# Routing weights of an expert layer: spread over the partitions by a DRAM round trip instead of TensorE products

## The reference

```
logits = gelu(xf @ w_r1 + b_r1) @ w_r2 + b_r2
probs = softmax(logits)
top_p, top_i = top_k(probs, 2);  top_p = top_p / sum(top_p)
v = 0;  integrated = xf
for _ in range(2):
    ctx = concat(integrated, v)
    shared: ctrl -> (x_shared, v_shared) by _inl
    per chosen expert: hidden = gelu(ctx @ w1[e] + b1[e]); ctrl = hidden @ w2[e] + b2[e]
                       (x_r, v_r) = _inl(ctrl, integrated, v, mu), weighted by top_p and summed
    x_next = sw * x_shared + (1 - sw) * x_r;  v_next likewise
    halt = sigmoid(gelu(x_next @ w_h1) @ w_h2); refined = gelu(x_next @ w_f1) @ w_f2
    integrated += halt * refined * integration_weight;  v = v_next

_inl: alpha, beta, gate = sigmoid, softplus, sigmoid of the thirds of ctrl
      v_next = alpha * v - beta * (x - mu);  x_next = x + 0.1 * gate * v_next
```

## Time and profile before

| | before |
|---|---|
| median of 3 runs | 743.63 us |
| lowest and highest | 735.77, 746.27 us |
| the profiled execution | 746.65 us |
| its span | 744.9 us |
| TensorE busy | 688.9 us (92%) |
| VectorE busy | 560.3 us (75%) |
| ScalarE busy | 489.3 us (66%) |
| GpSimd busy | 215.0 us (29%) |
| moved by DMA | 31.81 MB in 20987 packets |

### The profile page before, as it was taken

How to read it: one execution, slowest core, us unless ns; L and a number is a source line. 1 busy time by engine, 2 the same in 40 slices (tenths; PEclk the granted TensorE clock), 3 DMA queues, 4 the chain that set the end, 5 groups by cost and what they waited for, 6 DMA issues and landing times.

```text
span 744.9 us, 14725 instructions
## 1 busy us (share of the span) xinstructions
PE 688.9 (92%) x4872; PEld 368.8 (50%) x4872; DVE 560.3 (75%) x1749; ACT 489.3 (66%) x1342; POOL 215.0 (29%) x197
## 2 busy tenths in 40 slices
PE   6999999799999998999699999999979999989997
PEld 3655566466566432333245566655335665563332
DVE  4789898779998578677956999976038888845663
ACT  3778894389996688588857999834666666523201
POOL 2614662371444277336713032331000000000000
PEclk9899999899999989999899999999999999999999
DMA  5786000175000000000001600000000000000500
GB/s 204 158 253 259 1 3 1 33 162 127 3 2 2 2 0 1 0 2 0 0 22 45 128 2 2 2 29 1 0 0 1 1 2 1 0 1 1 227 2 28
DMA packets 20987, 31.81 MB, mean 43 GB/s; under 512 B 1648, under 2 KB 17968, under 8 KB 20272
## 3 DMA queue, kind: packets, MB, share of 16 engines
q1 hardware_dynamic: 20912, 30.86, 14.5%
HBM read 23.22 MB, written 7.63 MB: 41 GB/s over the span
## 4 chain that ended last, share of the span: by engine, by line
PE 69%; DVE 16%; ACT 8%; issue 5%; DMA 1%; POOL 1%; DVEq 0%; ACTq 0%; SPq 0%
PE bank L1137 12%; PE bank L1378 9%; DVE RING L1940 5%; PE bank L1408 4%; PE bank L1251 4%; PE bank L1540 4%; PE bank L1238 4%; DVE RING L1952 4%; PE bank L1327 4%; PE bank L1265 3%; PE bank L1527 3%; PE bank L1388 2%; PE bank L1740 2%; PE bank L1713 2%; PE bank L1158 2%
## 5 line engine op out<-in xcount | busy, mean ns | idle before, releaser
L938 ACT ACTIVATE RING<-RING,NMX 128x256 f32<-128x256 f32 x384 | 190.9, 500 | 25.8 <-DVE NMX L1940 24.1
L1940 DVE CUSTOM_DVE_ANT_0 RING<-bank,ADJM 128x256 f32<-128x256 f32 x384 | 145.5, 418 | 19.6 <-PE bank L1327 16.6
L1378 PE MATMUL bank<-W,RING 128*128 128x128 f32 x768 | 118.5, 287 | 5.4 <-ACT RING L950 5.1
L1378 PEld LDWEIGHTS bank<-W,RING 128*128 128x128 f32 x768 | 83.6, 144 | 52.9 <-ACT RING L938 41.5
L1952 DVE COPY RING<-bank 128x512 f32<-128x512 f32 x144 | 98.6, 686 | 5.6 <-PE bank L1378 5.2
L618 POOL TENSOR_TENSOR SUMS<-SUMS,small 128x8 f32<-128x8 f32 x36 | 59.2, 1644 | 127.0 <-ACT RING L938 127.0
L576 POOL TENSOR_TENSOR small<-small 128x2 f32<-128x2 f32 (+2 forms) x17 | 19.4, 1138 | 215.0 <-DVE small L1798 214.9
L938 ACT ACTIVATION_READ_ACCUMULATOR RING<-RING,NMX 128x1 f32 x384 | 72.8, 189 | 0.0
L852 ACT ACTIVATE RING<-bank,NMX 128x512 f32<-128x512 f32 x64 | 43.4, 684 | 39.1 <-DVE NMX L1882 29.2
L1882 DVE TENSOR_REDUCE NMX<-bank 128x1 f32<-128x512 f32 x64 | 39.8, 683 | 31.4 <-PE bank L1238 31.3
L1540 PE MATMUL bank<-ARENA,W 64*128 64x512 f32 x180 | 60.5, 669 | 2.3 <-DVE ARENA L2168 1.9
(11 more groups left out here) (265 smaller groups left out, 1241.3 us busy)
## 6 DMA issues: line engine op xcount, KB each, us to landing
ARENA<-scratch SPq DMA_DIRECT2D x12, 384.0 KB, 7.0
ARENA<-wrows SPq DMA_DIRECT2D x8, 512.0 KB, 7.5
scratch<-ARENA SPq DMA_DIRECT2D x18, 192.0 KB, 2.8
W<-in_weights SPq DMA_DIRECT2D x1, 2564.0 KB, 22.7
ARENA<-scratch SPq DMA_DIRECT2D x12, 192.0 KB, 3.7
scratch<-ARENA SPq DMA_DIRECT2D x18, 128.0 KB, 6.7
W<-in_weights SPq DMA_DIRECT2D x2, 1024.0 KB, 14.3
W<-in_weights SPq DMA_DIRECT2D x1, 1905.5 KB, 15.4
```

Of the source, the lines that this page charges most:

```text
L938: nc.scalar.activation(P_OF(n)[:, q * S:(q + 1) * S], S_OF(n)[:, q, :], ACT.Exp, bias=NMX[:, 2 * t + q:2 * t + q + 1], scale=-1.0, accum_o ...
L1378: mm = nc.tensor.transpose(bk[:, o:o + P], P_OF(n)[:, i:i + P], ident)
L1940: nc.vector.tensor_tensor_reduce(out=S_OF(n)[:, q, :], in0=SBANK(n)[:, q * S:(q + 1) * S], in1=ADJM[:, b, q, :], scale=-1.0, scalar=BIG, o ...
```

## The change

The three-part split, the selector products and their bank ring are gone. VectorE writes the weights once, in fp32, into `WT1` ordered by expert. One product with the identity turns them (64 rows of 128), `spread` is one copy of 64x128 into `WT1T`, SP writes that to a new DRAM tensor `wrows1` and reads rows back, broadcast over the 128 partitions: for each half-pass p and expert e one DMA of 512 tokens (128 x 512 fp32, 256 KB) into one of eight SBUF buffers `WROW1[e]`, 32 DMAs in all. The buffers are places whose contents are no longer needed (parameters of the first two attentions, `XN`, two of the bias matrices). For p of 1 and more each DMA waits until the multiply of the half-pass before has read the buffer. `first` and `scaled` read the weights from SBUF after waiting for `s_w1[e]`. The remaining entries of TensorE's list keep their order; `RB_AT` follows the count of banks.

```diff
-        WROW = RING[:, 12, :].bitcast(BF16)
-        WBF = small[:, 540:572].bitcast(BF16).rearrange("p (t e) -> p t e", t=NT)
+        WT1 = small[:, 640:704]
+        WT1T = RING[0:NE * NT, 12, 0:P]
+        WROW1 = ([w("wk0", i * 512, i * 512 + 512) for i in range(4)]
+                 + [XN[:, 4 * i:4 * i + 4, :].rearrange("p t d -> p (t d)") for i in range(2)]
+                 + [ADJ[:, i, :, :].rearrange("p q k -> p (q k)") for i in range(2)])
...
@@ block.sync
             write_keys(2)
+            sp.wait_ge(s_eb, RB_AT[2] - NC)
+            sp.dma_start(wrows1, WT1T).then_inc(s_w1dram, 16)
+            sp.wait_ge(s_w1dram, 16)
+            first_rows = wrows1.rearrange("(e t) j -> e (t j)", e=NE)
+            for p in range(2 * NC):
+                for e in range(NE):
+                    if p >= 1:
+                        sp.wait_ge(s_t1[p - 1] if p <= NC else s_tt[p - 1], nth(e))
+                    sp.dma_start(WROW1[e], first_rows[e:e + 1, half(p % NC)].to_broadcast([P, 512])).then_inc(s_w1[e], 16)
             sp.wait_ge(s_int, 2 * NC)
...
@@ block.tensor
                 pe.wait_ge(s_wt, 1)
-                for c in range(NC):
-                    bk = rb.fill(pe)
-                    for i in range(4):
-                        mm = nc.tensor.transpose(bk[0:3 * NE, i * P:(i + 1) * P], XN[:, 4 * c + i, 0:3 * NE], ident)
-                    mm.then_inc(s_fb, 1)
-
-            def weights(p, es):
-
-                for e in es:
-                    bk = rw.fill(pe, s_t1[p] if p < NC else s_tt[p], nth(e))
-                    nc.tensor.matmul(bk[:, :], ROWS[0:3 * NE, e * P:(e + 1) * P], WROW[0:3 * NE, half(p % NC)],
-                                     start=True, stop=True).then_inc(s_fw, 1)
+                bk = rb.fill(pe)
+                nc.tensor.matmul(bk[0:NE * NT, 0:P], WT1, ident, start=True, stop=True).then_inc(s_fb, 1)
...
             gates(0, (NE,))
-            pe.wait_ge(s_eb, rb.n)
-            weights(0, (0, 1))
             gates(0, (0, 1))
-            weights(0, (2, 3))
             gates(0, (2, 3, 4, 5))
-            weights(0, (4, 5))
...
@@ block.vector
-            link(nc.vector.scalar_tensor_tensor(WT8, EXPL, 1.0, SEL, ALU.add, ALU.mult))
-
-            for i in range(3):
-                link(nc.vector.tensor_copy(WBF, WT8))
-                part = nc.vector.tensor_copy(XN[:, :, NE * i:NE * (i + 1)], WBF)
-                if i < 2:
-                    link(part)
-                    link(nc.vector.tensor_tensor(WT8, WT8, XN[:, :, NE * i:NE * (i + 1)], ALU.subtract))
-            part.then_inc(s_wt, 1)
+            nc.vector.scalar_tensor_tensor(WT1.rearrange("p (e t) -> p t e", e=NE), EXPL, 1.0, SEL, ALU.add,
+                                           ALU.mult).then_inc(s_wt, 1)
 
             def spread():
 
-                for c in range(NC):
-                    nc.vector.tensor_copy(WROW[0:3 * NE, half(c)], rb.take(dve)[0:3 * NE, :]).then_inc(s_eb, 1)
+                nc.vector.tensor_copy(WT1T, rb.take(dve)[0:NE * NT, 0:P]).then_inc(s_eb, 1)
+
+            def weight(p, e):
+
+                dve.wait_ge(s_w1[e], 16 * (p + 1))
+                return WROW1[e]
...
             def first(p, es):
-                        wgt = rw.take(dve)
+                        wgt = weight(p, e)
                         dve.wait_ge(s_sp[p], nth(e))
                         nc.vector.tensor_tensor(sp, sp, wgt[:, :], ALU.mult).then_inc(s_t1[p], 1)
...
             def scaled(p, es):
-                        wgt = rw.take(dve)
+                        wgt = weight(p, e)
```

## The result

| | before | changed |
|---|---|---|
| median of 4 runs | 744.95 us | 752.61 us |
| lowest and highest | 735.77, 753.55 | 748.55, 756.49 |
| the profiled execution, its span | 746.65, 744.9 us | 756.49, 754.7 us |

A forecast was written before the change was run, and what follows sets the result against it. The routed layer was taken to have no single bound: ScalarE, VectorE and TensorE each fill one window. Terms +3.1 -3.9 -0.5 +1.5 +1.5 = +1.7 us gave 745 us from the median 743.63; range 734 to 757.

The forecast's parts named there:

- likeliest case: The whole kernel's time at 740 to 750 us, around the forecast of 745; chance 0.50.
- first rival: Pass 0: TensorE's pause for gate 5 grows, it slows down, lateness carries into pass 1; +9, 753 us; chance 0.22.
- late start: Pass 0: multiplies wait for rows through DRAM, end 4 us late, 0.9 of it slack; +3.1 us on ScalarE's path.
- contention alone: VectorE multiplies with both operands in SBUF slowed beside GpSimd: +1.5 us in pass 0 to 1, +1.5 in the last stage.
- products removed: TensorE's 32 weight products go: -3.9 us on the chain, and -0.5 for the waits tied to them.
- Weights made and spread: Layer start: weights copied at 260.3 us, first read 1.8 after the write, landing 3.3 later; first row at 265.7.
- What is late next: Pass 0: VectorE's late multiplies delay gate 5's bank and ScalarE's seventh gate; 4 us late, 0.9 slack, +3.1 us.
- Multiplies: 32 VectorE multiplies, now both operands in SBUF: about ten meet GpSimd, some 7 us together, +1.5 and +1.5 on the path.
- TensorE's clock: Behind the longer pause in pass 0, the slow stretch ends sooner (-3.3 us) or there are two (+3.3); taken as 0.
- Rows for later passes: Pass 1 onward: row reads are hidden behind other work and cost nothing; 3.3 us a pass if the cover were gone.
- The second: Rival: every one of the 32 multiplies meets GpSimd; +14 to +28 us, about 765 us; chance 0.08.
- The third, the uncoupling: Rival: TensorE and VectorE no longer wait over weight products; -8 us or so, 736 us; chance 0.17.

The follow-up runs named there:

- e11: Changed kernel with half-pass 0's rows read early from another tensor and all 32 multiplies reading a PSUM bank: layer 133.7 us, against 143.9 changed and 137.0 before.
- e2: Changed kernel, rows still late, but all 32 multiplies read a PSUM bank instead of the row: layer 137.5 us, whole 745.64 us, ratio 1.0021.
- e1: Changed kernel with half-pass 0's eight rows read early from a tensor already in DRAM, multiplies still from SBUF: layer 139.3 us, whole 745.55 us, ratio 1.0038.
- e6: Changed kernel with the turning product and the shared expert's product, which frees gate 5's bank, moved ahead: layer 143.5 us, whole 746.3 us, ratio 1.0075.
- e4: Kernel before without its 32 selector products and their waits, multiplies reading the banks as they are: layer 134.1 us, whole 740.16 us, ratio 0.9993.
- e3: Kernel before with all products and waits, but the 32 multiplies read their weight operand from SBUF: layer 142.7 us, whole 750.77 us, ratio 1.0095.
- e7: Changed kernel with softplus of half-pass 0 left in PSUM and two free banks given to the ring: layer 139.8 us, whole 749.02 us, ratio 0.9951.
- e8: Kernel before with the change in the second iteration only, the first keeping its products: layer 135.5 us, whole 738.77 us, ratio 0.9945.
- e5: Changed kernel with eight spare TensorE products between gates 4 and 5 of half-pass 0: layer 142.6 us, against 143.9 changed.
- e12: Changed kernel with eight banks, softplus of half-pass 0 left in PSUM, and turning and shared-expert products moved ahead: layer 139.3 us, whole 748.13 us, ratio 1.0079.

## Why the prediction was right or wrong

The median of 752.6 us lies in the range (734 to 757) and within 2%, as thought likeliest, but not in the likeliest case (740 to 750). It lies in the first rival's (750 to 758). The layer, forecast at +1.7 us, measures +6.9. No single step makes up the difference of 5.2 us; four were each too favourable by 0.8 to 2.2. The prediction's +3.1 for the late start held 1.5 of contention (the fourth multiply's end moved from 268.5 to 270.0), so to compare it with the runs I count 1.6 and 4.5:

| term | predicted | measured from e11 | off by |
|---|---|---|---|
| late start alone | +1.6 | +3.8 (e2) | 2.2 |
| contention alone | +4.5 | +5.6 (e1) | 1.1 |
| the two together | 0 | +0.8 | 0.8 |
| products removed | -4.4 | -3.3 (e11) | 1.1 |

- **Weights made and spread: nearly right.** The copy started at 260.4 us on the clock of the kernel before, predicted 260.3. The first read was issued 2.15 us after the write instead of 1.8, the first multiply came 3.3 us behind it as predicted, at 266.2 instead of 265.7. The reads of 256 KB bore out the value taken from the larger ones less half their increment. The estimate of 2.6 us by the Trainium skill (SBUF — State Buffer, the DMA setup-cost knee) is 0.7 below the 3.3 of the row.
- **What is late next: right in place, the largest miss in size.** The fourth multiply ended 4.8 us late (4 taken, 5.5 the bound); without contention, in e2, 3.0 us late (2.4 taken). The seventh gate came 5.0 us late (3.1 taken), so the 0.9 us counted as slack didn't help. Behind gate 5 stood beta 4, with the same wait (e6). How the 3.8 us divide between TensorE's wait and its slow passes stays open.
- **Products removed: right in sign, high in size.** In the first iteration their removal gave nothing by hidden(2) (e4), since TensorE ran refine(0) at a granted clock of 0.85 instead of 1.00.
- **Multiplies: the count right, the cost low.** Ten slow ones predicted and ten found; their excess is 8.0 us, 7 predicted. On the path up to hidden(2), 3.0 us were charged (1.5 of them in the late start) and 4.4 came (e11 to e1); 1.5 were charged in the last stage, where the second iteration as a whole gave 1.2. The prediction itself said that VectorE was busy 21.8 of 25 us in the window of pass 0 to 1. In e3 5.2 of 5.9 us of excess arrive at hidden(2), in e1 4.4 of 6.1.
- **TensorE's clock: taken as 0.** The stretch from refine(0) to hidden(2) is 1.2 us longer in e4 than before, with six passes at 4.61 us instead of 2.96; this lies inside the bounds of -3.3 to +3.3. The removed products bring it, for e4 has no late row and waits 1.4 us where the changed kernel waits 6.8. It is inside the terms of the table.
- **Rows for later passes: right.** No wait in half-passes 1 to 3, and in e11 no cost of the 32 DMAs shows.
- **The rivals.** The first has the right parts, and its 753 us meets the median partly by luck: the layer gives 6.9 of its 9 us, and it puts a second slow stretch at 3.3 us where the stretch at refine(0) shows 1.2 (e4). The second, every multiply contended, failed: 22 of 32 multiplies stayed below 0.8 us. The Trainium skill's rule (SBUF — State Buffer, Who interferes with whom) was right about which instructions contend: in e2 one PSUM operand brought all 32 back to 680 ns. The third, the uncoupling, failed: with the products and all their waits gone, e4 is 2.9 us shorter, where it counted 9.6.

## What to carry to other kernels

An operand's place is a cost of its own: moving a broadcast operand from PSUM to SBUF left the VectorE instruction as fast as it was while GpSimd was idle (684 against 679 ns) and still lost 5.7 us in e3 (137.0 to 142.7), because the instruction was slow beside GpSimd; leaving the other operand in PSUM, together with two more banks (e7), took back 4 us. Where an engine is nearly full in a window, charge most of its added time (here 5.2 of 5.9 us and 4.4 of 6.1). Work taken off TensorE can lower its granted clock, and so give back less than its own time (e4). And a round trip over DRAM (5.5 us here from copy to first use) belongs where the first use is that far away: the same edit in the second iteration alone shortened the layer (e8).

## What the runs showed of the hardware

- A VectorE instruction of 0.68 us with both operands in SBUF took up to 1.75 us beside GpSimd additions of 1.26 us, and these took up to 1.72 us beside it. With one operand in PSUM (e2) it took at most 0.69 us, and the additions beside it at most 1.28 us, one of 1.45 excepted that the kernel before has too.
- After a wait of 6.8 us TensorE needed 0.51 us per pass for ten passes, with a granted clock of 0.58 from 274.5 to 279.6 us (part at 1.2 GHz, part at 2.4); kept busy with spare products through most of that wait (e5) it needed 0.40, at 0.97 from 276.2 to 283.2 us. After a wait of only 1.4 us, without the selector products (e4), it needed 0.56.
- An instruction of VectorE with both operands in SBUF can take 1.73 or 0.73 us in the same place of two nearly equal kernels (`integrate(0)`, changed and e5), depending on where GpSimd's additions fall.
- 256 KB read from DRAM as one row of 2 KB broadcast over 128 partitions landed 3.0 us after its issue at the least, 3.3 in the median, 7.0 at the most; SP issued one in 0.32 us.
- The part of the kernel ahead of the changed layer took 242.7 to 251.4 us in fourteen traces, those of the two kernels and of e1 to e12. The granted clock of its stretch from 18 to 36 us was 0.84 in the trace of the kernel before and 0.72 in that of the changed one. Why it differs was not tried.
